# A two-layer graph kernel: edge counts gathered in windows of 12 destinations with four matmuls each, in place of 16 with five

## The chip, the core and the metric

The kernel runs on one NeuronCore of a Trainium2 chip. Its engines are TensorE (PE, with its weight loads PEld), VectorE (DVE), ScalarE (ACT), GpSimd (POOL) and SyncE (SP, which here only issues DMAs). The metric is the time of one execution on the device in microseconds (us).

## What is computed

`x` is 1250 x 1024, and the graph has 41250 edges (20000 random pairs in both directions and one loop per node), sorted by destination.

```python
h = jnp.maximum(_layernorm(x, axis=-1), 0.0)
# twice, with (Ws1, Wn1, b1) and (Ws2, Wn2, b2):
h_neigh = jax.ops.segment_sum(h[src], dst, num_segments=N_NODES)
h = h @ Ws + h_neigh @ Wn + b
# and at the end
x = x + h
```

The segment sum is done as a matrix product. `AT[s, d]` is the number of edges from source s to destination d; with it, h_neigh @ Wn is the transpose of AT times (h @ Wn). So the kernel first has to build AT, 1250 x 1250 small whole numbers, from the edge list.

## The kernel before

**Products.** A 32-bit operand is split in a high and a low part, and each product is three matmuls (high by high, high by low, low by high; `slab_products`, L1067). All are 128 x 128 weights by up to 512 columns.

**Stage 1** makes y1 = h @ Wn1 in 20 results (2 column halves by 10 node tiles), each of 8 slabs of 3 matmuls. The first 8 results are made while x is still being normalized and transposed. Then `stage1_order` goes on with the other 12 results and puts the count matmuls between their slabs: every 3 slabs a group of windows. PE, ACT, DVE and SP each walk an order that is derived from that list.

**From edge list to windows.** SP loads src and dst to `edge_ints`, 125 partitions of 330 edges (L422, L423). DVE splits src into its tile (src >> 7) and its place in the tile (src & 127) and writes f16 rows of 16 values to `edge_f16`: 5 edges a row, as 5 places, 5 tile keys, 5 destinations and one value that isn't used (`cast_edges`, L876 to L886). SP stores these 8250 rows of 32 bytes to `edge_rows` in DRAM (L432). Since the list is sorted, the edges of 16 neighbouring destinations (a window) are one run of rows, and the kernel must find where it begins: DVE compares the first destination of every third row with each window's start (`sample_edges`, L893), PE sums over partitions with 22 matmuls of 80 columns (L1107), and DVE turns the sums into row numbers (`find_rows`, L899 to L901). SP reads these and for each window copies 128 rows from DRAM to `window_edges`, one row per partition (`load_windows`, L442). A fetch is the 8 windows of one load of registers; fetches 0 to 6 are issued in a row, the others between the loads of the second half's weight slabs. POOL makes `pair_m` and `pair_key` from each fetch with four instructions (L602 to L608); a destination outside the window gets a key that matches nothing.

**Counting.** For a pair of windows DVE makes two tables of zeros and ones: `hot_m` (for each of 5 edges per partition, 128 source places; L922) and `hot_n` (10 source tiles by 16 destinations = 160 columns; L924), in a ring of `HOT` = 4 pairs. PE multiplies them: 5 matmuls of 160 columns per window add up to its counts (`count_window`, L1059). Three windows share a PSUM bank, and when such a group is done ACT copies 480 columns to AT (`save_counts`, L735).

In the end DVE and PE sum all counts. If the sum isn't 41250, a slow path that can hold any edge list builds AT anew; `flag` decides, and every engine branches on it before stage 2.

**Later stages.** Stage 2 (L1155, L1163) makes the transposed first layer, PE's L1192 makes the second layer's products by a scheme of sums of blocks, and L1208 multiplies by AT again.

The functions that the diff touches:

## Time and profile before

| | |
|---|---|
| Runs | 663.59, 658.75, 662.05 us, median 662.05 |
| Profiled execution | 660.24 us, span of its trace 658.4 us |
| PE busy in the span | 637.4 us (97%), mean granted clock 0.997 |
| Stretch with the counts, 75.86 to 160.02 us | PE 84.12, weight loads 68.69, DVE 68.34, ACT 27.56, POOL 14.51 us busy |
| Count matmuls | 400 of 128x160, 400 weight loads of 128x128, f16 |

The profiled execution lies inside the spread of the three runs. In the trace a line's "busy" is the time covered by its instructions; the matmuls overlap one another, so the time from one start to the next is shorter than the duration of one. "Idle before" is time in which the engine had nothing to run, with what ended it behind the arrow. PE's idle time adds up to 21 us; nearly all of it lies in the first 23 us, around 171 us and 247 us, and at the end.

### The profile page before, as it was taken

Reading aid. Unit: us, or ns where it says so; the run is one execution under the profiler, and the core shown is the slowest. Engines: PE = TensorE matmul, PEld = TensorE weight load, DVE = VectorE, ACT = ScalarE, POOL = GpSimd, SP = SyncE. Lnnn points to the kernel's source line nnn. Section 1 sums busy time; section 2 is a strip of 40 time slices with the busy share of each in tenths; the row PEclk is TensorE's granted clock in tenths of the full one; section 3 lists DMA queues with packets and bytes.
Section 4 is the critical chain, followed back from the end, with each engine's and each line's share of the span. In section 5 each row is a group of like instructions: output and inputs, shape, how many; then the busy total and the mean of one; then the engine's idle time right before and its main releaser. Section 6 shows DMA issues by size and latency. Waiting matters only on the chain.

```text
span 658.4 us, 8500 instructions
## 1 busy us (share of the span) xinstructions
PE 637.4 (97%) x3280; PEld 555.4 (84%) x3280; DVE 280.3 (43%) x386; ACT 175.7 (27%) x292; POOL 212.4 (32%) x201
## 2 busy tenths in 40 slices
PE   3799999999899999999999999999999999999997
PEld 2688778887799999999999988888888888887885
DVE  2653799783111211120122383325287987611111
ACT  5444343222213313323233121311334433100000
POOL 5432335000247656775680157103214013000000
PEclk9899999999999999999999999999999999999999
DMA  8622330001446766566755766455422243011111
GB/s 276 216 40 56 85 112 33 33 33 62 137 135 196 258 222 232 199 223 202 259 216 176 246 223 231 157 159 160 127 81 69 76 160 96 33 54 59 61 48 62
DMA packets 62724, 90.61 MB, mean 138 GB/s; under 512 B 16545, under 2 KB 34987, under 8 KB 62678
## 3 DMA queue, kind: packets, MB, share of 16 engines
q1 hardware_dynamic: 42342, 76.08, 34.6%
q10 hardware_dynamic: 20336, 13.91, 6.8%
q8 instruction: 30, 0.49, 0.3%
q14 instruction: 16, 0.13, 0.1%
HBM read 58.49 MB, written 31.48 MB: 137 GB/s over the span
## 4 chain that ended last, share of the span: by engine, by line
PE 62%; DMA 1%; DVE 0%; ACT 0%; POOL 0%; issue 0%; SPq 0%; DVEq 0%
PE PS L1192 29%; PE PS L1208 14%; PE PS L1155 10%; PE PS L1163 9%; DMA quarters<-ws_in 1%; DVE W_st L979 0%; POOL prep_sum L617 0%; ACT W_st L728 0%; DVE s L1047 0%; ACT prep L779 0%; SPq L487 0%; DVEq L1046 0%
## 5 line engine op out<-in xcount | busy, mean ns | idle before, releaser
L1192 PE MATMUL PS<-right,left 128*128 128x512 f32 x840 | 190.6, 389 | 0.0
L1192 PEld LDWEIGHTS PS<-right,left 128*128 128x128 f32 x840 | 157.8, 188 | 32.6
L1067 PE MATMUL PS<-W,HT 128*128 128x512 f32 (+1 forms) x480 | 123.0, 406 | 2.5 <-issue 2.4
L1155 PE MATMUL PS<-HT,W_st 128*128 128x416 f32 (+1 forms) x576 | 110.4, 352 | 2.4 <-issue 1.7
L1155 PEld LDWEIGHTS PS<-HT,W_st 128*128 128x128 f32 x576 | 107.9, 188 | 4.0 <-issue 3.1
L1067 PEld LDWEIGHTS PS<-W,HT 128*128 128x128 f32 (+1 forms) x480 | 87.8, 190 | 22.0 <-issue 2.8
L1163 PE MATMUL PS<-AT,y_st 128*128 128x416 f32 (+2 forms) x480 | 92.1, 351 | 0.0
L1163 PEld LDWEIGHTS PS<-AT,y_st 128*128 128x128 f32 (+1 forms) x480 | 90.0, 188 | 0.7
L650 POOL TENSOR_TENSOR left_sum<-h1T 128x640 f32<-128x640 f32 x24 | 41.9, 1746 | 149.9 <-PE PS L1192 120.0
L617 POOL TENSOR_TENSOR prep_sum<-quarters 128x512 f32<-128x512 f32 x40 | 51.6, 1293 | 102.8 <-PE PS L1067 62.8
L1208 PE MATMUL PS<-y_high,AT 128*128 128x512 f32 (+1 forms) x200 | 78.4, 392 | 0.0
L1208 PE MATMUL PS<-y_low,AT 128*128 128x512 f32 (+1 forms) x200 | 78.4, 392 | 0.0
L622 POOL TENSOR_TENSOR prep<-prep_sum,prep 128x512 fp32r<-128x512 f32 x40 | 60.7, 1520 | 25.9 <-ACT prep L779 25.9
L979 DVE TENSOR_TENSOR W_st<-W_st_raw,W_st 128x1024 fp32r<-128x1024 f32 x8 | 14.4, 1798 | 85.2 <-ACT W_st L728 85.2
L1208 PEld LDWEIGHTS PS<-y_low,AT 128*128 128x128 f32 (+1 forms) x200 | 37.2, 186 | 8.8
L1047 DVE TENSOR_TENSOR s<-s,PS 128x512 f32<-128x512 f32 (+1 forms) x20 | 13.7, 687 | 72.0 <-PE PS L1208 72.0
L1208 PEld LDWEIGHTS PS<-y_high,AT 128*128 128x128 f32 (+1 forms) x200 | 37.1, 185 | 8.7
L982 DVE TENSOR_TENSOR y_st<-y_st_raw,y_st 128x1152 fp32r<-128x1152 f32 x8 | 10.9, 1358 | 77.7 <-ACT y_st L765 77.7
L779 ACT ACTIVATE prep<-prep_sum 128x512 fp32r<-128x512 f32 x40 | 23.6, 624 | 64.8 <-POOL prep_sum L617 35.7
L1009 DVE TENSOR_TENSOR s<-s,PS 128x512 f32<-128x512 f32 (+1 forms) x60 | 37.2, 681 | 6.5 <-PE PS L1192 4.5
L924 DVE TENSOR_TENSOR hot_n<-iota_n,pair_key 128x1600 f16<-128x1600 f16 x40 | 39.4, 985 | 0.0
L922 DVE TENSOR_TENSOR hot_m<-iota_m,pair_m 128x1280 f16<-128x1280 f16 x40 | 33.0, 826 | 9.3 <-PE PS L1059 9.2
(79 smaller groups left out, 452.1 us busy)
## 6 DMA issues: line engine op xcount, KB each, us to landing
sums_dram<-prep SPq DMA_DIRECT2D x40, 512.0 KB, 2.9
right<-sums_dram SPq DMA_DIRECT2D x40, 512.0 KB, 3.5
y_dram<-y_out ACTq DMA_DIRECT2D x18, 256.0 KB, 2.1
y_st_raw<-y_dram ACTq DMA_DIRECT2D x8, 576.0 KB
s<-x_in SPq DMA_DIRECT2D x18, 256.0 KB
out<-s SPq DMA_DIRECT2D x18, 256.0 KB
W_raw<-wn_in SPq DMA_DIRECT2D x16, 256.0 KB, 4.0
xin<-x_in SPq DMA_DIRECT2D x8, 512.0 KB, 12.2
```

Of the source, the lines that this page charges most:

```text
L617: nc.gpsimd.tensor_tensor(prep_sum[:, i % PREP, LO, :], quarters[:, QUARTERS.index(a), :], quarters[:, QUARTERS.index(b), :], op).then_inc ...
L622: nc.gpsimd.tensor_tensor(prep[:, i % PREP, LO, :], prep_sum[:, i % PREP, LO, :], prep[:, i % PREP, HI, :].bitcast(F32), ALU.subtract).the ...
L650: nc.gpsimd.tensor_tensor(left_sum[:, k, LO, :], h1_block(*a, k), h1_block(*b, k), op).then_inc(left_summed, 1)
L779: nc.scalar.activation(prep[:, i % PREP, HI, :], prep_sum[:, i % PREP, LO, :], ACT.Copy).then_inc(prep_hi, 1)
L922: nc.vector.tensor_tensor(hot_m[:, u % HOT, :, :, :], iota_m[:, :, :].unsqueeze(1).to_broadcast([P, ROW, P, 2]), pair_m[:, u, :, :].unsque ...
L924: nc.vector.tensor_tensor(hot_n[:, u % HOT, :, :, :], iota_n[:, :, :].unsqueeze(1).to_broadcast([P, ROW, NCOL, 2]), pair_key[:, u, :, :].u ...
L1009: nc.vector.tensor_tensor(c, c, PS[:r, BANKS2[g % 8], :], op).then_inc(dve_evicted, 1)
L1067: ins = nc.tensor.matmul(PS[:r, bank, :], HT[:, a, k, t * P:t * P + r], W[:, k, b, :], start=first and m == 0, stop=last and m == 2)
L1155: ins = nc.tensor.matmul(PS[:, banks[c], 0:w_], W_st[:, a, k, :], HT[:, b, k, o_:o_ + w_], start=k == 0 and m == 0, stop=False)
L1163: ins = nc.tensor.matmul(PS[:, banks[c], 0:w_], y_st[:r, part, s, :].bitcast(dt), AT[:r, s, o_:o_ + w_].bitcast(dt), start=False, stop=s = ...
L1192: ins = nc.tensor.matmul(PS[:, BANKS2[g % 8], :], left[:, k, a, i * P:(i + 1) * P], right[:, KB - 1 - k, b, :], start=k == 0 and j == 0, s ...
L1208: ins = nc.tensor.matmul(PS[:rows_of(t), BANKS2[g % 8], :], AT[:r, s, t * P:t * P + rows_of(t)].bitcast(dt), y.bitcast(dt), start=s == 0 a ...
```

## The change

A window is 12 destinations, and a row holds 4 edges. A window's counts are 4 matmuls of 120 columns (10 source tiles by 12). There are 106 windows and 53 pairs, in groups of 4 windows (480 columns, one bank), 27 groups as before. The last window is empty, since pairs need an even number. Rows of 4 edges don't divide 41250 evenly, so the list is padded to 123 partitions of 84 rows: DVE fills the end with destination 2047 before SP loads, and each of src and dst comes in two DMAs. A fetch is 10 windows (the last one 6), 11 fetches, of which 7 are issued at first and 4 after the last weight slab of the second half. The ring has 5 pairs. `samples` now shares its memory with `src_parts`.

```diff
--- before.py
+++ after.py
@@ -21,25 +21,28 @@
 HI, LO = 0, 1
 PRODUCTS = ((HI, HI), (HI, LO), (LO, HI))
 CH = ((0, 416), (416, 416), (832, 418))
-WIN = 16
-NW = NPAD // WIN
-WPT = P // WIN
-ROW = 5
+WIN = 12
+NW = 2 * -(-N // (2 * WIN))
+FETCH = 10
+NFETCH = -(-NW // FETCH)
+ROW = 4
 ROWX = 16
-EROWS = E // ROW
 SAMPLE = 3
-EP = 125
-EPP = E // EP
-RPP = EPP // ROW
+EP = 123
+RPP = 84
+EPP = RPP * ROW
+TAIL = E - (EP - 1) * EPP
+EROWS = EP * RPP
+NOWHERE = 2047
 NSAMP = RPP // SAMPLE
 KEY = WIN + 2
-ANY = 8
+ANY = 10
 NCOL = NT * WIN
-GROUP = 3
+GROUP = 4
 NG = -(-NW // GROUP)
-HOT = 4
+HOT = 5
 NS = NW // 2
-SPW = WPT // 2
+SPF = FETCH // 2
 SLAB_LAG = 6
 EPS = 1e-5
 EARLY = 8
@@ -151,6 +154,11 @@
     return w // GROUP
 
 
+def fetched(a):
+
+    return range(a * FETCH, min((a + 1) * FETCH, NW))
+
+
 def last_of_group(w):
     return w % GROUP == GROUP - 1 or w == NW - 1
 
@@ -194,16 +202,13 @@
 def sync_order():
 
     ends = y1_ends()
-    yield ("windows", EARLY - 1)
     for p, event in enumerate(stage1_order()):
         if event[:2] == ("y1", NT - 1):
             yield ("slab", event[2])
-            if event[2] == 2:
-                yield ("windows", EARLY)
         if event == ("y1", 2 * NT - 1, 6):
             yield ("w_st", 0)
         if p in ends and ends[p] == NT - 1:
-            yield ("windows", EARLY + 1)
+            yield from (("windows", a) for a in range(EARLY - 1, NFETCH))
 
 
 def scalar_order():
@@ -276,8 +281,8 @@
         ident = at("ident", [P, P], F32, o); o += up(P * 4)
         edge_f16 = at("edge_f16", [EP, RPP, ROWX], F16, o); o += up(RPP * ROWX * 2)
         edge_ints = at("edge_ints", [EP, 2, EPP], I32, o); o += up(2 * EPP * 4)
-        src_parts = at("src_parts", [EP, 2, EPP], I32, o); o += up(2 * EPP * 4)
-        samples = at("samples", [EP, NSAMP, NW], F16, o); o += up(NSAMP * NW * 2)
+        src_parts = at("src_parts", [EP, 2, EPP], I32, o)
+        samples = at("samples", [EP, NSAMP, NW], F16, o); o += up(max(NSAMP * NW * 2, 2 * EPP * 4))
         pad_row = at("pad_row", [P, ROWX], F16, o); o += up(ROWX * 2)
         assert o <= W0, o - W0
 
@@ -337,13 +342,13 @@
 
 
 
-        edges_in = sem("edges_in"); consts_in = sem("consts_in"); b2_in = sem("b2_in")
+        edges_padded = sem("edges_padded"); edges_in = sem("edges_in"); consts_in = sem("consts_in"); b2_in = sem("b2_in")
         x_in_t = [sem(f"x_in_{t}") for t in range(NT)]; x_in_first = sem("x_in_first")
         setup = sem("setup"); pool_self = sem("pool_self"); dve_self = sem("dve_self"); act_self = sem("act_self")
 
         src_split = sem("src_split"); edges_cast = sem("edges_cast"); rows_saved = sem("rows_saved")
         sampled = sem("sampled"); counted = sem("counted"); row_found = sem("row_found")
-        windows_in = [sem(f"windows_in_{a}") for a in range(NT)]
+        windows_in = [sem(f"windows_in_{a}") for a in range(NFETCH)]
         clipped = sem("clipped"); rebased = sem("rebased")
 
         warm = sem("warm"); var_ready = sem("var_ready"); norm_self = sem("norm_self"); norm_ready = sem("norm_ready")
@@ -419,8 +424,12 @@
             load_x_tile(1)
             for k in range(2, KF):
                 load_w(wn1, 0, k)
-            sp.dma_start(edge_ints[:, 0, :], src.rearrange("(p e) -> p e", p=EP)).then_inc(edges_in, 16)
-            sp.dma_start(edge_ints[:, 1, :], dst.rearrange("(p e) -> p e", p=EP)).then_inc(edges_in, 16)
+            sp.wait_ge(edges_padded, 1)
+            for part, ends in enumerate((src, dst)):
+                sp.dma_start(edge_ints[0:EP - 1, part, :],
+                             ends[0:(EP - 1) * EPP].rearrange("(p e) -> p e", p=EP - 1)).then_inc(edges_in, 16)
+                sp.dma_start(edge_ints[EP - 1:EP, part, 0:TAIL],
+                             ends[(EP - 1) * EPP:E].rearrange("(p e) -> p e", p=1)).then_inc(edges_in, 16)
             for t in range(2, NT):
                 load_x_tile(t)
             with nc.allow_non_contiguous_dma("4 KB bias as a column for each feature tile"):
@@ -436,11 +445,10 @@
             def load_windows(a):
 
                 _, rows = nc.values_load_multi_w_load_instructions(
-                    row_i[0:1, a * WPT:(a + 1) * WPT], engines=(mybir.EngineType.SP,), min_val=0, max_val=EROWS,
+                    row_i[0:1, fetched(a)[0]:fetched(a)[-1] + 1], engines=(mybir.EngineType.SP,), min_val=0, max_val=EROWS,
                     skip_runtime_bounds_check_because="a count of sampled edges times 3, less 3 and at least 0: at most EROWS - 3")
-                for j in range(WPT):
-                    sp.dma_start(window_edges[:, a * WPT + j, :],
-                                 edge_rows[bass.ds(rows[j], P), :]).then_inc(windows_in[a], 16)
+                for w, row in zip(fetched(a), rows):
+                    sp.dma_start(window_edges[:, w, :], edge_rows[bass.ds(row, P), :]).then_inc(windows_in[a], 16)
 
             sp.wait_ge(rows_saved, 32)
             sp.wait_ge(row_found, 1)
@@ -588,19 +596,20 @@
                                    allow_small_or_imprecise_dtypes=True).then_inc(iotas, 1)
 
 
-            for a in range(NT):
-                pool.wait_ge(windows_in[a], WPT * 16)
-                rows = window_edges[:, a * WPT:(a + 1) * WPT, :]
+            for a in range(NFETCH):
+                pool.wait_ge(windows_in[a], len(fetched(a)) * 16)
+                these = slice(fetched(a)[0], fetched(a)[-1] + 1)
+                rows = window_edges[:, these, :]
                 place = rows[:, :, 2 * ROW:3 * ROW]
 
                 def in_pairs(field):
                     return rows[:, :, field * ROW:(field + 1) * ROW].rearrange("p (u e) i -> p u e i", e=2)
 
                 def pairs(tile):
-                    return tile[:, a * SPW:(a + 1) * SPW, :, :].rearrange("p u i e -> p u e i")
+                    return tile[:, these.start // 2:these.stop // 2, :, :].rearrange("p u i e -> p u e i")
 
                 nc.gpsimd.tensor_copy(pairs(pair_m), in_pairs(0))
-                nc.gpsimd.tensor_tensor(place, place, win_start[:, a * WPT:(a + 1) * WPT].unsqueeze(2).to_broadcast([P, WPT, ROW]),
+                nc.gpsimd.tensor_tensor(place, place, win_start[:, these].unsqueeze(2).to_broadcast([P, len(fetched(a)), ROW]),
                                         ALU.subtract).then_inc(clipped, 1)
                 pool.wait_ge(clipped, 2 * a + 1)
                 nc.gpsimd.tensor_scalar(place, place, -1.0, float(WIN), ALU.max, ALU.min).then_inc(clipped, 1)
@@ -872,7 +881,7 @@
 
             def cast_edges():
 
-                dve.wait_ge(edges_in, 32)
+                dve.wait_ge(edges_in, 64)
                 nc.vector.tensor_scalar(src_parts[:, 0, :], edge_ints[:, 0, :], P - 1, None, ALU.bitwise_and).then_inc(src_split, 1)
                 nc.vector.tensor_scalar(src_parts[:, 1, :], edge_ints[:, 0, :], P.bit_length() - 1, None,
                                         ALU.logical_shift_right).then_inc(src_split, 1)
@@ -887,7 +896,7 @@
                                         ALU.mult).then_inc(edges_cast, 1)
 
             def sample_edges():
-                dve.wait_ge(edges_cast, 1)
+                dve.wait_ge(edges_cast, 3)
                 dve.wait_ge(setup, 3)
                 first = edge_f16[:, :, 2 * ROW:2 * ROW + 1].rearrange("p (q s) o -> p q (s o)", s=SAMPLE)[:, :, 0:1]
                 nc.vector.tensor_tensor(samples[:, :, :], win_start[:EP, :].unsqueeze(1).to_broadcast([EP, NSAMP, NW]),
@@ -900,6 +909,7 @@
                 chain(nc.vector.tensor_scalar(row_f[:, :], row_f[:, :], 0.0, None, ALU.max))
                 nc.vector.tensor_copy(row_i[:, :], row_f[:, :]).then_inc(row_found, 1)
 
+            nc.vector.memset(edge_ints[96:EP, :, TAIL:EPP], NOWHERE).then_inc(edges_padded, 1)
             statistics(0)
             statistics(1)
             low_of_h(0)
@@ -917,7 +927,7 @@
 
             dve.wait_ge(iotas, 2)
             def one_hots(u):
-                dve.wait_ge(rebased, u // SPW + 1)
+                dve.wait_ge(rebased, u // SPF + 1)
                 dve.wait_ge(hot_free, 2 * u + 2)
                 nc.vector.tensor_tensor(hot_m[:, u % HOT, :, :, :], iota_m[:, :, :].unsqueeze(1).to_broadcast([P, ROW, P, 2]),
                                         pair_m[:, u, :, :].unsqueeze(2).to_broadcast([P, ROW, P, 2]), ALU.is_equal)
```

Where the counts stand on PE, in the middle of results 8 and 9 (results with 98 rows are the last tile's). Before:

```order
L1067 MATMUL PS<-W,HT 128x512 x3
L1067 MATMUL PS<-W,HT 98x512 x3
L1067 MATMUL PS<-W,HT 128x512 x3
L1059 MATMUL PS<-hot_n,hot_m 128x160 x15
L1067 MATMUL PS<-W,HT 98x512 x3
L1067 MATMUL PS<-W,HT 128x512 x3
L1067 MATMUL PS<-W,HT 98x512 x3
```

and now:

```order
L1077 MATMUL PS<-W,HT 128x512 x3
L1077 MATMUL PS<-W,HT 98x512 x3
L1077 MATMUL PS<-W,HT 128x512 x3
L1069 MATMUL PS<-hot_n,hot_m 128x120 x16
L1077 MATMUL PS<-W,HT 98x512 x3
L1077 MATMUL PS<-W,HT 128x512 x3
L1077 MATMUL PS<-W,HT 98x512 x3
```

The groups keep their places between the slabs of L1067 (now L1077); each has one matmul more, of 40 columns less.

The SP queue at the edge list, between the first weight slabs and the other x tiles. Before:

```order
L408 DMA W_raw<-wn_in 128x512 x6
L422 DMA edge_ints<-src_in 125x330
L423 DMA edge_ints<-dst_in 125x330
L413 DMA xin<-x_in 128x1024 x7
L413 DMA xin<-x_in 98x1024
L427 DMA b_sb<-b_in 128x8x1
L430 DMA edge_rows<-pad_row 128x16
L432 DMA edge_rows<-edge_f_66 125x1056
```

and now:

```order
L413 DMA W_raw<-wn_in 128x512 x6
L429 DMA edge_ints<-src_in 122x336
L431 DMA edge_ints<-src_in 1x258
L429 DMA edge_ints<-dst_in 122x336
L431 DMA edge_ints<-dst_in 1x258
L418 DMA xin<-x_in 128x1024 x7
L418 DMA xin<-x_in 98x1024
L436 DMA b_sb<-b_in 128x8x1
L439 DMA edge_rows<-pad_row 128x16
L441 DMA edge_rows<-edge_f_66 123x1344
```

Two DMAs of one partition each stand ahead of x tiles 2 to 9, and the first edge DMA waits for DVE's padding.

The DVE around the first weight slabs of the second half (L931, now L941), where it also makes the tables. Before:

```order
L922 TENSOR_TENSOR hot_m<-iota_m,pair_m 128x1280
L924 TENSOR_TENSOR hot_n<-iota_n,pair_key 128x1600
L922 TENSOR_TENSOR hot_m<-iota_m,pair_m 128x1280
L924 TENSOR_TENSOR hot_n<-iota_n,pair_key 128x1600
L931 TENSOR_TENSOR W<-W_raw,W 128x512
L922 TENSOR_TENSOR hot_m<-iota_m,pair_m 128x1280
L924 TENSOR_TENSOR hot_n<-iota_n,pair_key 128x1600
L931 TENSOR_TENSOR W<-W_raw,W 128x512
L922 TENSOR_TENSOR hot_m<-iota_m,pair_m 128x1280
L924 TENSOR_TENSOR hot_n<-iota_n,pair_key 128x1600
L931 TENSOR_TENSOR W<-W_raw,W 128x512
L922 TENSOR_TENSOR hot_m<-iota_m,pair_m 128x1280
```

and now:

```order
L932 TENSOR_TENSOR hot_m<-iota_m,pair_m 128x1024
L934 TENSOR_TENSOR hot_n<-iota_n,pair_key 128x960
L941 TENSOR_TENSOR W<-W_raw,W 128x512
L932 TENSOR_TENSOR hot_m<-iota_m,pair_m 128x1024
L934 TENSOR_TENSOR hot_n<-iota_n,pair_key 128x960
L941 TENSOR_TENSOR W<-W_raw,W 128x512
L932 TENSOR_TENSOR hot_m<-iota_m,pair_m 128x1024
L934 TENSOR_TENSOR hot_n<-iota_n,pair_key 128x960
L941 TENSOR_TENSOR W<-W_raw,W 128x512
L932 TENSOR_TENSOR hot_m<-iota_m,pair_m 128x1024
L934 TENSOR_TENSOR hot_n<-iota_n,pair_key 128x960
L932 TENSOR_TENSOR hot_m<-iota_m,pair_m 128x1024
```

The first slabs stand at the same places, and from the fourth on a pair more comes before a slab. The tables have 1024 and 960 values a partition where they had 1280 and 1600.

## Rows read from the trace of the kernel before

**Rows 1.** The page, sections 1 and 4: busy shares and the chain of waits by line
```profile
PE 637.4 (97%) x3280; PEld 555.4 (84%) x3280; DVE 280.3 (43%) x386; ACT 175.7 (27%) x292; POOL 212.4 (32%) x201
...
PE PS L1192 29%; PE PS L1208 14%; PE PS L1155 10%; PE PS L1163 9%; DMA quarters<-ws_in 1%; DVE W_st L979 0%; POOL prep_sum L617 0%; ACT W_st L728 0%; DVE s L1047 0%; ACT prep L779 0%; SPq L487 0%; DVEq L1046 0%
```

**Rows 2.** Windows by stage: length, busy us (x instructions), PEclk, DMA share, GB/s
```profile
75.80:160.00 84.20, 84.16 (x635) 68.67 (x635) 68.40 (x84) 27.56 (x70) 14.51 (x8) 1.00 0.17 55
```

**Rows 3.** PE timeline, first and last count groups: start us, us, op xcount
```profile
75.86 1.25 PE L1059 MATMUL PS<-hot_n,hot_m 128*128 128x160 f16 x15
76.90 2.33 PE L1067 MATMUL PS<-W,HT 128*128 128x512 f32 x9
79.07 1.25 PE L1059 MATMUL PS<-hot_n,hot_m 128*128 128x160 f16 x15
...
89.69 2.64 PE L1067 MATMUL PS<-W,HT 128*128 128x512 f32 x9
...
159.34 0.89 PE L1059 MATMUL PS<-hot_n,hot_m 128*128 128x160 f16 x10
```

**Rows 4.** Groups by line and shape, engine PE: xcount, busy us, mean ns, idle before
```profile
L1067 PE MATMUL PS<-W,HT 128*128 128x512 f32 x432 | 111.8, 407 | 2.5 <-issue 2.4
...
L1059 PE MATMUL PS<-hot_n,hot_m 128*128 128x160 f16 x400 | 33.3, 234 | 0.0
...
L1107 PE MATMUL PS<-samples,ones_f 125*1 125x80 f16 x22 | 0.9, 201 | 0.0
```

**Rows 5.** The same view of the weight loads, engine PEld: mean ns behind the busy us
```profile
L1059 PEld LDWEIGHTS PS<-hot_n,hot_m 128*128 128x128 f16 x400 | 27.9, 97 | 7.3 <-issue 6.4 <-DVE hot_n L924 0.8
...
L1107 PEld LDWEIGHTS PS<-samples,ones_f 125*1 125x1 f16 x22 | 0.8, 86 | 0.4 <-issue 0.4
```

**Rows 6.** PE timeline before the counts, from 22 to 39 us
```profile
22.28 1.10 PE L1093 MATMUL PS<-ident,hbuf 128*128 128x128 f32 x8 [3.58 <-ACT hbuf L685]
23.13 5.94 PE L1067 MATMUL PS<-W,HT 128*128 128x512 f32 x18
29.00 0.95 PE L1107 MATMUL PS<-samples,ones_f 125*1 125x80 f16 x22
...
32.16 5.72 PE L1067 MATMUL PS<-W,HT 128*128 128x512 f32 x24
```

**Rows 7.** DVE timeline: early steps, then the start of the one-hots
```profile
18.14 0.69 DVE L859 BATCH_NORM_STATS2 stats<-xin 128x6 f32<-128x512 f32 x1 [4.79 <-DMA xin<-x_in]
...
22.21 1.97 DVE L893 TENSOR_TENSOR samples<-win_start,edge_f 125x1760 f16<-125x1760 f16 x1
...
72.03 0.92 DVE L922 TENSOR_TENSOR hot_m<-iota_m,pair_m 128x1280 f16<-128x1280 f16 x1
...
75.49 0.81 DVE L922 TENSOR_TENSOR hot_m<-iota_m,pair_m 128x1280 f16<-128x1280 f16 x1
76.22 0.98 DVE L924 TENSOR_TENSOR hot_n<-iota_n,pair_key 128x1600 f16<-128x1600 f16 x1
77.12 0.81 DVE L922 TENSOR_TENSOR hot_m<-iota_m,pair_m 128x1280 f16<-128x1280 f16 x1
...
80.40 0.68 DVE L931 TENSOR_TENSOR W<-W_raw,W 128x512 fp32r<-128x512 f32 x1
```

**Rows 8.** POOL timeline: first of the four instructions of the last fetch
```profile
96.67 8.80 POOL L602 COPY pair_m<-window_edges 128x40 f16<-128x40 f16 x1 [7.66 <-DMA window_edges<-edge_rows]
```

**Rows 9.** SP queue timeline: DMA issues, start us, us to issue
```profile
7.45 0.36 SPq L423 DMA_DIRECT2D edge_ints<-dst_in  x1
...
31.69 38.82 SPq L442 DMA_DIRECT2D window_edges<-edge_rows  x64
74.66 4.23 SPq L408 DMA_DIRECT2D W_raw<-wn_in  x3
```

**Rows 10.** DMA issues: KB each, median us from issue to landing
```profile
xin<-x_in SPq DMA_DIRECT2D x8, 512.0 KB, 12.2
```

**Rows 11.** ACT timeline: high part of the first second-half weight slab
```profile
77.70 0.62 ACT L660 ACTIVATE W<-W_raw 128x512 fp32r<-128x512 f32 x1
```

## The prediction

> **What bounds the kernel now.** The windows by stage come first: from 75.8 to 160.0 us PE is busy 84.16 of 84.20 us at full clock, DVE 68.40, ACT 27.56, POOL 14.51 [rows 2]. In the whole span PE is busy 97%, and the chain of waits, from its beginning at 235 us to the end, is nearly all later matmuls [rows 1]. It never reaches the stretch that is changed, so it can't tell what that is worth. What does tell it is that PE idles nowhere in the stretch, and that the work behind it is PE's too, or is released by PE. So a microsecond of PE time taken out moves everything behind it forward, as long as nobody else becomes late.
>
> Then the PE timeline: groups of 15 count matmuls and 9 slab matmuls alternate, a period of 79.07 - 75.86 = 3.21 us [rows 3]. What matters is the pitch, from one start to the next, not the duration. A run of n lasts (n-1) pitches and one duration. At 160 columns, with 0.234 us for one [rows 4]: the runs of 15 and 10 differ by 1.25 - 0.89 = 0.36 us for 5 more, so the pitch is 72 ns [rows 3]. At 80 columns, the sampling: (0.95 - 0.20)/21 = 36 ns [rows 4, 6]. At 512 columns: (5.72 - 0.41)/23 = 231 ns [rows 4, 6]. The three lie on one line of 0.45 ns a column with nothing to speak of as a fixed part. So these pairs of load and matmul are bound by the columns that stream through, not by the weights.
>
> **Count matmuls.** Removed: 400 of 160 columns at 72 ns, 28.8 us. Added: 424 of 120 columns. The trace has no 120-column matmul on 128 columns of f16 weights. The line between 80 and 160 columns gives 36 + 40 x 0.45 = 54 ns, so 22.9 us, a gain of 5.9. By group: 15 x 72 = 1.08 us becomes 16 x 54 = 0.86, 27 groups at the same places among the same slabs, and the period goes from 3.21 to 2.99. Bounds: the 36 ns of the 80-column row would be below even streaming; 72 ns holds if the load of 128 f16 weight columns needs as long as that. The 80-column row can't exclude it, as its weights are one column wide. I take 54, because the f16 load of 128 columns lasts 97 ns against 86 for one column [rows 5], so all but 11 ns of it is latency that the next load overlaps.
>
> Here a rule speaks against the change. The Trainium skill (TensorE: Matmul & The Clock Gate, Back-to-back issue gap) gives about 81 ns for a sustained pair of load and matmul at 128 columns. The trace disagrees: 72 ns at 160 columns. By the rule the sum would be 424 x 81 = 34.3 us, 5.5 more than now; it is a rival below.
>
> **Sampling.** 22 matmuls of 80 columns become 28 of 106. By the same line 106 columns take 36 + 26 x 0.45 = 48 ns: 1.34 us against 0.79, on PE and in no one's shadow, **+0.55 us**. DVE's comparison grows from 1760 to 2968 values: 1.97 us [rows 7] becomes 3.3. Before, it ended at 24.2 and PE reached the sampling at 29.00 [rows 6, 7], so 1.3 us more costs nothing; without that 4.8 us cover it would cost all of it. The next tile's statistics move back with it, but PE needs that tile only after 31 us.
>
> **The front of the SP queue.** Two more DMA issues of 0.36 us each, some 0.45 with their gaps [rows 9], stand ahead of x tiles 2 to 9. Tile 2 matters: DVE waits 4.79 us for it, until 18.14 [rows 7], and PE waits 3.58 us until 22.28 for what is made of it [rows 6]. Later PE is full. So a later landing of tile 2 costs its whole delay: 0.9 us if issue decides, nothing if the DMA engines are the bottleneck. A tile needs 12.2 us from issue to landing [rows 10], so the queue is deep in bytes and these hardly change. I take **+0.2**, ends 0 and 0.9. DVE's padding write runs while it waits for the first x tile, and SP asks for it only near 6.9 us: nothing.
>
> **Windows.** 64 DMAs take 38.82 us to issue, 0.607 each [rows 9]. Seven fetches of 10 are 42.5 us. They begin at 31.69 + 0.55 and end near 74.8; the first second-half weight load went out at 74.66 [rows 9], because it waits for PE anyway. The cover is just used up and each further microsecond moves the weights back. DVE's one-hots stand behind these weights. The other 36 windows come after PE ends results 8 and 9, four periods after the first group, about 88.5 us; at 0.607 they are out by 111, the first ten by 95. DVE can't reach their first pair (35) before 72 + 35 x 1.15 + 8 x 0.7 = 118. POOL's first copy of a fetch can last 8.80 us while DVE works without a pause [rows 8]. Even with that it is done by 105. Nothing.
>
> **One-hots.** Next-start times give 0.73 us for 1280 values and 0.90 for 1600 [rows 7]: 0.53 ns a value and 0.05 fixed. A pair of 1024 and 960 values is 0.59 + 0.56 = 1.15 us, 53 pairs 61 us in place of 40 x 1.63 = 65. PE uses a pair in 1.49 us. DVE starts four microseconds ahead. It will wait for the first weight slab: ACT makes that at 77.7 after the first group's eviction [rows 11], now near 78.1, so DVE stands from about 77.9 to 78.8. Pair 5 is then ready near 80.6, and PE wants it with the third group at 76.4 + 2 x 2.99 = 82.4. Cost nothing; without the cover of 1.8 us, what is over. The 0.3 us that the slab run at 89.69 has over its neighbours [rows 3] stay.
>
> ACT evicts the same 480 columns 27 times. The later stages have the same instructions.
>
> **The sum.** -5.9 + 0.55 + 0.2 = **-5.15 us** on the profiled execution's 660.24 gives 655.1. That execution lies 1.8 under the median of the runs, 662.05, and from the median it would be 656.9. I take **656**, between the two.
>
> **Rivals.**
> *The weight load sets the pitch* (slower than before). Place: the count groups. The sum changes sign where 424 pitches are 28.8 - 0.75 = 28.05 us, at 66 ns. With the pitch left at 72 ns the counts take 30.5 us, +1.7 + 0.75 = +2.4: 662.6 on the profile's base, 664.5 on the median's. For it: no row with this load under 120 columns. Against: 97 against 86 ns. Somewhere between, at 62 ns, it would be -1.8. Chance 0.10.
>
> *The page's pitch of 81 ns*: as a mechanism the same, a longer load, +5.5 + 0.75 = +6.2, 667.4. The row at 72 ns speaks flatly against it. Chance 0.02.
>
> *DVE becomes the bound.* If a table costs the same whatever its length, a pair stays at 1.63 us: 72 + 53 x 1.63 + 8 x 0.7 = 164 us, against 160.0 for the end of the counts before. That is +4, 665. It decides from (154.8 - 72 - 5.6)/53 = 1.46 us a pair. The two rows at 0.73 and 0.90 us say that length counts. A weaker form, weights late behind the windows on SP, costs 1 or 2 us. Chance 0.06.
>
> *Tile 2 late by the issue*: -4.5, 656.7. Chance 0.08.
>
> *The change doesn't do its work*: a window whose edges exceed 512 places would send the kernel to its slow path, 10 rounds of 336 edges with three matmuls of up to 512 columns, over 2000 us more. In the given list the furthest edge of a window is the 470th of 512 places (the 593rd of 640 before), and 2047 matches no window. Chance under 0.01.
>
> The forecast keeps 0.73. Its own uncertainty is 2 ns of pitch (0.8 us) and the base, 4.8 us between the runs. The range of **652.5 to 662.5** holds it, the late tile and half of the floor cases. About 1% is what this measurement can tell from no change, 6.6 us. My gain is 0.8%, so **within 1%** has 0.77, **faster by over 1%** 0.19 (the forecast with a kind base, or DVE's shorter tables freeing something unseen), **slower by over 1%** 0.04 (the page's rule, DVE bound at its worst, the slow path).
>
> **What will show it.** The 120-column runs of 16 in the PE timeline: (duration - one)/15 near 54 ns, period near 2.99 us, counts over some 5.4 us earlier after a start 0.75 later. DVE's tables near 0.65 us each with the wait before the hot tables on PE. The first weight load near 74.8 to 75. The sampling near 1.5 us as a run. I am wrong if the runs of 16 last over 1.2 us (load-bound), if PE shows idle time before L1069 with the hot tables as releaser, or if PE's 3.58 us wait grew.

## The result and the profile after

The changed kernel takes 668.31 us (median of 6 runs, 666.0 to 672.61) against 662.11 for the kernel before. The ratio of the runs is **1.0109**, 95% interval 1.0077 to 1.014 (the two medians alone give 1.0094): slower by about 1%, where 656 us and a gain of 0.8% were forecast, and outside the range of 652.5 to 662.5. The profiled execution has a span of 666.0 us, 7.6 more than before. Three executions in the experiments below, one of e12 (912.48 us at a granted clock of 0.66) and two of the kernel before beside e7 to e12 (671.23 and 2273.64 us), are longer than the others of their kernel, and the ratios leave them out.

First the page of the profile of the changed kernel, section 1 (busy us, share, instructions):

```profile
PE 637.4 (96%) x3310; PEld 553.7 (83%) x3310; DVE 277.3 (42%) x413; ACT 175.4 (26%) x292; POOL 213.8 (32%) x205
```

PE is as busy as before, 637.4 us [rows 1], so the 7.6 us are idle time on PE. What the count matmuls saved in busy time is filled up again, by the longer sampling and by stretches at half clock. Its timeline says where (start us, us, op; in brackets the idle time before, and what ended it):

```profile
26.38 1.97 PE L1103 MATMUL PS<-ident,hbuf 128*128 128x128 f32 x8 [6.04 <-ACT hbuf L694]
...
30.72 0.97 PE L1077 MATMUL PS<-W,HT 128*128 128x512 f32 x3 [0.22 <-POOL W L568]
...
34.21 1.52 PE L1117 MATMUL PS<-samples,ones_f 123*1 123x106 f16 x28
...
81.83 1.04 PE L1069 MATMUL PS<-hot_n,hot_m 128*128 128x120 f16 x16
...
84.83 1.05 PE L1069 MATMUL PS<-hot_n,hot_m 128*128 128x120 f16 x16
...
91.65 0.98 PE L1069 MATMUL PS<-hot_n,hot_m 128*128 128x120 f16 x8 [3.20 <-DVE hot_n L934]
92.39 3.40 PE L1077 MATMUL PS<-W,HT 128*128 128x512 f32 x9
```

Three things are to be seen, besides the counts.

1. The transposes of tile 2 begin at 26.38 us, where they began at 22.28 [rows 6]: PE waited for `hbuf`, 6.04 us in place of 3.58, and the eight then last 1.97 us in place of 1.10, at half clock. After them there are new short waits for POOL, and the sampling starts at 34.21 in place of 29.00. The counts begin at 81.83, not 75.86 [rows 3]: **6.0 us late**.
2. A run of 16 lasts 1.04 us. With 0.22 for one, the pitch is (1.04 - 0.22)/15 = 55 ns, and the period is 84.83 - 81.83 = 3.00 us. Both are what was forecast (54 ns, 2.99 us).
3. In the third group PE stops for **3.20 us** for `hot_n`. Then the clock is at half: 9 slab matmuls last 3.40 us in place of 2.31.

The last count starts at 165.03 us. In the windows, the stretch in which PE waited shows the granted clock:

```profile
88.00:91.60 3.60, 0.45 (x8) 0.28 (x6) 1.87 (x4) 1.81 (x4) 0.61 (x2) 0.96 0.92 304
91.60:94.60 3.00, 2.95 (x13) 2.40 (x14) 3.00 (x6) 2.33 (x5) 0.00 (x0) 0.50 0.13 48
```

(The columns are the stretch and its length, busy us of PE, PEld, DVE, ACT and POOL with their instructions, PEclk, DMA share, GB/s.) PE was busy for 0.45 us of 3.6; for the next three microseconds the granted clock was 0.50, which is 1.2 GHz.

**Why the counts begin late.** The SP queue of the changed kernel:

```profile
6.63 0.61 SPq L429 DMA_DIRECT2D edge_ints<-src_in  x1
7.28 2.13 SPq L431 DMA_DIRECT2D edge_ints<-src_in  x1
9.45 0.25 SPq L429 DMA_DIRECT2D edge_ints<-dst_in  x1
9.74 3.22 SPq L431 DMA_DIRECT2D edge_ints<-dst_in  x1
13.01 3.81 SPq L418 DMA_DIRECT2D xin<-x_in  x8
...
37.95 48.29 SPq L451 DMA_DIRECT2D window_edges<-edge_rows  x70
86.29 12.86 SPq L413 DMA_DIRECT2D W_raw<-wn_in  x8
```

The DMAs behind the two of 122 partitions are held for 2.13 and 3.22 us. The x tiles go out from 13.01, not 7.85. DVE's first use of tile 2, and the two instructions that met next:

```profile
22.24 0.69 DVE L868 BATCH_NORM_STATS2 stats<-xin 128x6 f32<-128x512 f32 x1 [8.68 <-DMA xin<-x_in]
...
26.29 3.23 DVE L902 TENSOR_TENSOR samples<-win_start,edge_f 123x2968 f16<-123x2968 f16 x1
```

```profile
25.00 6.90 POOL L568 TENSOR_TENSOR W<-W_raw,W 128x512 fp32r<-128x512 f32 x3
```

Tile 2 is used at 22.24 us, 4.10 later than at 18.14 [rows 7]. And POOL's last three weight subtractions last 6.90 us, where before they took 5.66:

```profile
20.90 5.66 POOL L560 TENSOR_TENSOR W<-W_raw,W 128x512 fp32r<-128x512 f32 x3
```

PE's last nine products before the sampling stand behind the last of these slabs. They are released by POOL at 31.96 us, 0.06 us after it ends, and the sampling starts 2.31 us after POOL ends; before it was 2.44.

**Why PE stops.** The 70 windows take 48.29 us to issue in place of the 42.5 that I had worked out, from a start 6.3 us later than before. So the first second-half weights go out at 86.29 us, 4.5 after the first count, where before they went out 1.2 ahead of it [rows 3, 9]. What loads the row numbers into SP's registers (duration in ns, min/median/max; first and last start): the second and third load of the changed kernel, and then all ten of the kernel before.

```profile
L447 SPq TENSOR_LOAD <-row_i x1: 2076/2076/2076, 43.0 to 43.0; - x1
```

```profile
L447 SPq TENSOR_LOAD <-row_i x1: 947/947/947, 50.8 to 50.8; - x1
```

```profile
L438 SPq TENSOR_LOAD <-row_i x10: 521/528/740, 30.8 to 89.2; - x10
```

DVE stands in its order behind those weights:

```profile
83.46 0.65 DVE L934 TENSOR_TENSOR hot_n<-iota_n,pair_key 128x960 f16<-128x960 f16 x1
89.73 0.69 DVE L941 TENSOR_TENSOR W<-W_raw,W 128x512 fp32r<-128x512 f32 x1 [5.63 <-ACT W L669]
90.34 0.68 DVE L932 TENSOR_TENSOR hot_m<-iota_m,pair_m 128x1024 f16<-128x1024 f16 x1
90.94 0.65 DVE L934 TENSOR_TENSOR hot_n<-iota_n,pair_key 128x960 f16<-128x960 f16 x1
```

Five pairs were ready at 84.1 us. The sixth comes after 5.63 us of waiting for `W`, and PE runs out of tables. A pair takes 0.60 us from the start of one table to that of the next, and 0.57 more, so 1.17, near the forecast 1.15.

### The profile page after: what moved, and what is told of

Same layout as the page of the kernel before. It is cut to its first block, busy times and chain, and to the rows that moved or that the text cites. A ratio compares the mean times of both kernels' runs of the same rounds, so it can differ in the third digit from the quotient of the medians.

```text
span 666.0 us, 8685 instructions
## 1 busy us (share of the span) xinstructions
PE 637.4 (96%) x3310; PEld 553.7 (83%) x3310; DVE 277.3 (42%) x413; ACT 175.4 (26%) x292; POOL 213.8 (32%) x205
## 4 chain that ended last, share of the span: by engine, by line
PE 54%; POOL 1%; DMA 1%; DVE 0%; ACT 0%; SPq 0%; issue 0%; POOLq 0%; DVEq 0%
PE PS L1202 29%; PE PS L1218 14%; PE PS L1165 6%; PE PS L1173 5%; DMA quarters<-wn_in 1%; POOL prep L631 0%; POOL prep_sum L626 0%; DVE W_st L989 0%; SPq L482 0%; ACT W_st L737 0%; DVE s L1057 0%; ACT prep L788 0%; SPq L495 0%; POOLq L625 0%; DVEq L1056 0%
## 5 line engine op out<-in xcount | busy, mean ns | idle before, releaser
L1077 PE MATMUL PS<-W,HT 128*128 128x512 f32 (+1 forms) x480 | 124.7, 409 | 2.9 <-issue 2.4
L1077 PEld LDWEIGHTS PS<-W,HT 128*128 128x128 f32 (+1 forms) x480 | 88.6, 192 | 23.4 <-issue 2.8
L631 POOL TENSOR_TENSOR prep<-prep_sum,prep 128x512 fp32r<-128x512 f32 x40 | 57.7, 1446 | 28.8 <-ACT prep L788 28.6
L932 DVE TENSOR_TENSOR hot_m<-iota_m,pair_m 128x1024 f16<-128x1024 f16 x53 | 36.5, 690 | 6.7 <-PE PS L1069 6.6
L934 DVE TENSOR_TENSOR hot_n<-iota_n,pair_key 128x960 f16<-128x960 f16 x53 | 34.8, 656 | 0.0
```

The lines of the kernel that those rows point to most:

```text
L631: nc.gpsimd.tensor_tensor(prep[:, i % PREP, LO, :], prep_sum[:, i % PREP, LO, :], prep[:, i % PREP, HI, :].bitcast(F32), ALU.subtract).the ...
L932: nc.vector.tensor_tensor(hot_m[:, u % HOT, :, :, :], iota_m[:, :, :].unsqueeze(1).to_broadcast([P, ROW, P, 2]), pair_m[:, u, :, :].unsque ...
L934: nc.vector.tensor_tensor(hot_n[:, u % HOT, :, :, :], iota_n[:, :, :].unsqueeze(1).to_broadcast([P, ROW, NCOL, 2]), pair_key[:, u, :, :].u ...
L1077: ins = nc.tensor.matmul(PS[:r, bank, :], HT[:, a, k, t * P:t * P + r], W[:, k, b, :], start=first and m == 0, stop=last and m == 2)
```

## The experiments

Ratios are to the kernel before on the same chip, with 95% intervals; like the first one, they can differ from the ratio of the two medians, by up to 0.2%. "Repaired" is short for one DMA each for src and dst and fetches of 8.

### e1 and e2: undo one part each

e1 pads inside each of 125 partitions, so each of src and dst comes in one DMA.

```diff
-EP = 123
+EP = 125
...
-                sp.dma_start(edge_ints[0:EP - 1, part, :], ends[0:(EP - 1) * EPP]...)
-                sp.dma_start(edge_ints[EP - 1:EP, part, 0:TAIL], ends[(EP - 1) * EPP:E]...)
+                sp.dma_start(edge_ints[:, part, 0:REAL], ends...)   # REAL = 330
...
-            nc.vector.memset(edge_ints[96:EP, :, TAIL:EPP], NOWHERE)
+            nc.vector.memset(edge_ints[:, :, REAL:EPP], NOWHERE)
```

> The changed kernel with its edge list padded in another way: 125 partitions of 330 edges as before, each with 6 places of padding behind them (one write of DVE), so that src and dst come in one DMA each and no DMA of one partition is left. Windows, matmuls and fetches are the changed kernel's. Theory 'front': the two one-partition DMAs hold SP's queue for 2.13 and 3.22 us, x tile 2 lands 4.1 us late, and PE begins the counts 6.0 us late. Then the counts begin near 76.6 us (81.83 in the changed kernel), and PE still stalls some 3 us in the third group, as the windows' issue still takes 48 us: about 5.4 us less than the changed kernel, 663. Rival 'more edge work' (larger sampling and casts, more bytes): no change, the counts begin near 82 us, 668.

Measured: 664.05 us, ratio 1.0053 (1.0023 to 1.0082). The x tiles in the SP queue, and PE's timeline:

```profile
7.51 4.45 SPq L418 DMA_DIRECT2D xin<-x_in  x8
```

```profile
30.19 1.52 PE L1115 MATMUL PS<-samples,ones_f 125*1 125x106 f16 x28
...
77.64 1.04 PE L1067 MATMUL PS<-hot_n,hot_m 128*128 128x120 f16 x16
...
87.14 0.98 PE L1067 MATMUL PS<-hot_n,hot_m 128*128 128x120 f16 x8 [2.87 <-DVE hot_n L932]
```

The x tiles go out at 7.51 us and the counts begin at 77.64, 4.2 earlier than in the changed kernel: the front theory holds for 4.2 of its 6.0 us, where 5.2 were expected. The sampling still starts 1.2 us later than at 29.00 [rows 6], though its tile is not late. The stall is there, 2.87 us.

e2 changes one number.

```diff
-FETCH = 10
+FETCH = 8
```

> The changed kernel with fetches of 8 windows (14 fetches, 7 of them first) in place of 10. The one-partition DMAs stay. Theory 'row numbers': SP loads 10 row numbers in 0.94 or 2.1 us where 8 took 0.53, so the windows go out late, the second half's first weights behind them too, and DVE with its tables waits for those weights. Then the loads are back at 0.53, the first 56 windows are out in about 34 us (by 72), the first weight load waits for PE again (near 80.5), PE's 3.2 us stall and the half-clock stretch behind it go: 5.3 us less than the changed kernel, 663, and the counts begin at 81.8 as there. Rival 'DVE is the bound': the stall stays.

Measured: 661.86 us, ratio 1.0014 (0.9986 to 1.0043). The loads of row numbers, the SP queue and PE:

```profile
L447 SPq TENSOR_LOAD <-row_i x11: 522/527/732, 36.5 to 109.4; - x11
```

```profile
37.41 33.81 SPq L451 DMA_DIRECT2D window_edges<-edge_rows  x56
80.38 13.76 SPq L413 DMA_DIRECT2D W_raw<-wn_in  x8
```

```profile
81.58 1.04 PE L1069 MATMUL PS<-hot_n,hot_m 128*128 128x120 f16 x16
...
160.02 0.61 PE L1069 MATMUL PS<-hot_n,hot_m 128*128 128x120 f16 x8
```

The loads are back at 0.53 us, SP waits for PE again, and there is no stall: the last count starts at 160.02, 5.0 us before that of the changed kernel, with the start of the counts all but unmoved (81.58 against 81.83). DVE is no bound. The gain is of the size that the row-number theory gave, but the edit changes two things: with fetches of 8, the seven fetches ahead of the weights hold 56 windows, not 70. At this run's own rate, 33.81/56 = 0.604 us a window, 70 would take 42.3 us (an estimate) and be out near 79.7, just ahead of 80.38. So by that estimate the short loads would have been enough, but no run had 70 windows in front and loads of 8. The next run keeps the 70.

### e6: is it ten numbers, or where they lie?

```diff
-        row_i = at("row_i", [1, NW], I32, o)
+        row_i = at("row_i", [1, NFETCH * 16], I32, o)
...
-                    row_i[0:1, fetched(a)[0]:fetched(a)[-1] + 1], ...
+                    row_i[0:1, a * 16:a * 16 + len(fetched(a))], ...
...
```

> The changed kernel with fetches of 10 windows, but the 10 row numbers of each fetch stored at a multiple of 64 bytes (16 places a fetch, written by two copies on DVE). In the changed kernel the loads of 10 numbers alternate between 2.1 us (starts at an odd multiple of 40 bytes) and 0.94 (at an even one). If the start address makes the 2.1 us, all loads take 0.94 or less, the 70 windows go out in about 43 us instead of 48.3, by 81, the weights come in time and PE's stall of 3.2 us mostly goes: 664. If only the number 10 counts, they stay between 0.94 and 2.1 and so does the time, 668.

Measured: 664.13 us, ratio 1.0056 (1.0027 to 1.0086). The loads and the SP queue:

```profile
L447 SPq TENSOR_LOAD <-row_i x11: 714/945/1623, 36.6 to 117.2; - x11
```

```profile
38.00 44.71 SPq L451 DMA_DIRECT2D window_edges<-edge_rows  x70
82.76 12.33 SPq L413 DMA_DIRECT2D W_raw<-wn_in  x8
```

So both count. Ten numbers at a multiple of 64 bytes take 0.95 us (the median; the shortest is the last fetch of six, the first takes 1.16 and one behind the weights 1.62), eight take 0.53. In the changed kernel all five loads that start at an odd multiple of 40 bytes take over 2 us (three times 2.07 to 2.08, and 3.51 and 2.70 behind the weights), and the six others 0.94 to 1.17. With the same 70 windows in front, the issue is 3.6 us shorter, and PE's waits for hot tables shrink from 3.20 to 0.76 us in all. This is the run that shows the row numbers as the cause of most of the stall, with only the place of the numbers changed.

### e4 and e5: what holds the queue?

e4 puts the two one-partition DMAs at the head of the queue.

```diff
+            for part, ends in enumerate((src, dst)):
+                sp.dma_start(edge_ints[EP - 1:EP, part, 0:TAIL], ends[(EP - 1) * EPP:E]...)
             sp.dma_start(xin[:, 0, 0:HALF], x[0:P, 0:HALF]).then_inc(x_in_first, 16)
...
-                sp.dma_start(edge_ints[EP - 1:EP, part, 0:TAIL], ends[(EP - 1) * EPP:E]...)
```

> The changed kernel with its two one-partition DMAs as the very first in SP's queue, where no transfer is under way. Why do they hold the queue? If by themselves (a cost of the form), the first x tile lands 5 us later than at 3.4, and the time stays near 668 or above. If because they meet a backlog of the W transfers, they take about 0.4 us each, x tile 0 lands at 4.2, x tile 2 near 19, the counts begin near 77.5: 664 (the windows' stall stays).

Measured: 669.17 us, ratio 1.0130 (1.0093 to 1.0167). A miss. The SP queue:

```profile
0.75 0.35 SPq L421 DMA_DIRECT2D edge_ints<-src_in  x1
...
8.26 1.84 SPq L432 DMA_DIRECT2D edge_ints<-dst_in  x1
10.15 7.46 SPq L418 DMA_DIRECT2D xin<-x_in  x8
```

The one-partition DMAs are cheap there, 0.35 us for the first, as the backlog theory has it. But the delay did not go: now the second DMA of 122 partitions is held for 1.84 us, and the eight x tiles take 7.46 to issue. What came behind a DMA of 122 partitions was held in both orders. The one-partition DMAs were only the first to stand there.

e5 splits the last partition off in the kernel before: 124 partitions and 1.

```diff
-            sp.dma_start(edge_ints[:, 0, :], src.rearrange("(p e) -> p e", p=EP))...
-            sp.dma_start(edge_ints[:, 1, :], dst.rearrange("(p e) -> p e", p=EP))...
+            for part, ends in enumerate((src, dst)):
+                sp.dma_start(edge_ints[0:EP - 1, part, :], ends[0:(EP - 1) * EPP]...)
+                sp.dma_start(edge_ints[EP - 1:EP, part, :], ends[(EP - 1) * EPP:E]...)
```

> The kernel before, with src and dst each loaded in two DMAs: 124 partitions of 330 edges, and the last partition by itself. Nothing else is changed. Theory 'front': the two one-partition DMAs alone take 5 us of SP's queue, x tile 2 lands near 22, and the kernel is 4 to 5.5 us slower, 667. Rival: the 5 us come from the padding or the other sizes; then no change, 662.

Measured: 661.37 us, ratio 1.0000 (0.9968 to 1.0031): no change. My first front theory, that the one-partition DMAs cost 5 us by their form, falls. All four issues took 0.25 to 0.48 us.

### e7: 122 partitions by themselves

The kernel before with 122 and 3 partitions.

```diff
...
+                sp.dma_start(edge_ints[0:122, part, :], ends[0:122 * EPP]...)
+                sp.dma_start(edge_ints[122:EP, part, :], ends[122 * EPP:E]...)
```

> The kernel before, with src and dst each loaded in two DMAs: 122 partitions and the other 3. No matmul or window is changed. The run with 124 and 1 partitions held nothing up (four issues of 0.25 to 0.48 us), and with the one-partition DMAs first in the queue it was still the DMA behind a 122-partition one that waited. New theory: the partition count decides over how many DMA engines a transfer is spread; 122 = 2 x 61 leaves two, whose queues fill, and the next issues wait. The Trainium skill (DMA: Bandwidth & Descriptors, How many engines) says so: the largest number up to 16 that divides the count. From the changed kernel's trace, as a mechanism here: the issues behind the 122-partition ones take 2 to 3 us, x tile 2 is used near 22 (18.1 before), the counts begin near 80, and the kernel is 3.5 to 5 us slower, 664 to 665. Rival: it needs the 1344-byte rows or one-partition transfers as well; then no change, 660.5.

Measured: 664.95 us, ratio 1.0055 (1.0028 to 1.0081). The SP queue of e7, then the windows from 12 to 14 us of e7 and of e5:

```profile
7.67 1.73 SPq L425 DMA_DIRECT2D edge_ints<-src_in  x1
...
9.74 3.28 SPq L425 DMA_DIRECT2D edge_ints<-dst_in  x1
13.07 3.89 SPq L413 DMA_DIRECT2D xin<-x_in  x8
```

```profile
12.00:14.00 2.00, 0.83 (x2) 0.76 (x3) 1.07 (x1) 1.98 (x3) 2.00 (x2) 1.00 0.15 53
```

```profile
12.00:14.00 2.00, 0.00 (x0) 0.00 (x0) 1.19 (x1) 2.00 (x3) 2.00 (x2) 1.00 1.02 308
```

The same is seen, 1.73 and 3.28 us, with 1320-byte rows, without padding and without a one-partition transfer. The x tiles go out at 13.07, tile 2 is used 4.16 us late, and the counts begin at 81.31 us, 5.45 late. Most of what is over came with the clock: PE waited 6.77 us for that tile, and the granted clock was 0.50 from 24 to 32 us. In the stretch from 12 to 14 us the DMA engines are nearly idle (the two numbers at the end: share and GB/s), while with 124 + 1 partitions, in the second row, they are full (1.02). The Trainium skill (DMA: Bandwidth & Descriptors, section Why a DMA increments its semaphore by 16 and not by 1) says that a transfer is spread over the largest number of engines up to 16 that divides the partition count; by this rule that is 2 for 122, 4 for 124, 5 for 125. The traces agree as far as they go: the share of 0.15 is 2.4 of 16 engines at work, and the issue waits. They don't name the engines of a packet, so the count of two, and that it is why the issue waits, isn't shown by a trace.

### e9: POOL beside DVE

In the repaired kernel:

```diff
             low_of_h(1)
-            sample_edges()
             for t in range(3, NT):
                 statistics(t)
                 low_of_h(t - 1)
                 if t == 3:
+                    sample_edges()
                     find_rows()
```

> The repaired kernel (one DMA each for src and dst, fetches of 8) with DVE's comparison of samples moved behind the next tile's statistics and low part. In the changed kernels three weight subtractions on POOL take 6.90 us while the comparison of 3.23 us runs, 5.66 beside one of 1.97, and PE waits for them. Theory 'POOL beside DVE': with the comparison at 25.5 to 28.8 the three take 3.8 us, PE isn't held by POOL, waits for the samples instead, and reaches the sampling near 28.9 in place of 30.2 to 31.2: 1 to 2 us less than the repaired kernel, 659. Rival: the subtractions are long by themselves there; then PE comes later, 661 or more.

Measured: 657.62 us, ratio 0.9963 (0.9934 to 0.9991). POOL, and PE:

```profile
21.52 3.85 POOL L566 TENSOR_TENSOR W<-W_raw,W 128x512 fp32r<-128x512 f32 x3
```

```profile
29.52 1.52 PE L1115 MATMUL PS<-samples,ones_f 125*1 125x106 f16 x28 [1.40 <-DVE samples L900]
...
77.05 1.04 PE L1067 MATMUL PS<-hot_n,hot_m 128*128 128x120 f16 x16
```

The three subtractions take 3.85 us with DVE's comparison out of their way; 5.66 us beside one of 1.97, 6.90 beside one of 3.23. All but 0.2 us of the comparison's length is added to them (1.81 and 3.05 us), so POOL made next to no headway while it ran. In the Trainium skill (GPSIMD Engine Reference, section Specifications) the two share their SBUF interfaces, with contention where a DVE instruction has two SBUF inputs, as this one has; the trace agrees. PE now waits 1.40 us for the samples instead. What the edit gains over the repaired kernel is small at best, as e10 and e11 show below.

### e3, e8, e10, e11: both repairs, and what became of the gain

e3 has the edits of e1 and e2 together:

```diff
-EP = 123
+EP = 125
-FETCH = 10
+FETCH = 8
```

> Both edits together: one DMA each for src and dst, and fetches of 8. Front and row numbers together explain the miss: the counts begin near 76.6 us, no stall of PE, the count matmuls 5.9 us shorter: 657 to 658, 0.7% under the kernel before. If something else is lost in the later stages (PE idles 1.45 us at 305 us in the changed kernel and not before), it stays 1.5 us above that, 659.

Measured: 660.64 us, ratio 0.9998 (0.9974 to 1.0023), a miss by about 3 us; no stall in the counts, which begin at 78.65 and end 2.5 us before those of the kernel before. So 2.5 us of gain at that point, and none at the end in these rounds. Two tests of where it went. e8, the kernel before with more rows in DRAM:

```diff
-    edge_rows = nc.dram_tensor("edge_rows", (EROWS + P + 3, ROWX), F16, kind="Internal").ap()
+    edge_rows = nc.dram_tensor("edge_rows", (10332 + P + 3, ROWX), F16, kind="Internal").ap()
```

> The kernel before with 2082 unused rows behind edge_rows in DRAM, so that the tensors behind it (y1_dram, sums_dram) move to the addresses that they have in the changed kernel. Nothing else is changed. Where did the gain of the repaired kernel go? Its counts end 2.5 us before those of the kernel before, and the whole isn't shorter: stage 2 idles more for W_st, and the stores of the prepared sums land in 3.0 to 3.2 us in place of 2.9. Theory 'addresses': this kernel is 1.5 to 3 us slower, 662 to 663. Rival 'chance or phase': no change, 660.5.

Measured: 660.91 us, ratio 0.9996 (0.9972 to 1.002). And e10, e3 with the tensor of the rows declared behind the one of the sums:

```diff
-    edge_rows = nc.dram_tensor("edge_rows", (EROWS + P + 3, ROWX), F16, kind="Internal").ap()
...
+    edge_rows = nc.dram_tensor("edge_rows", (EROWS + P + 3, ROWX), F16, kind="Internal").ap()   # now after sums_dram
```

> The repaired kernel with edge_rows declared behind y1_dram and sums_dram, which keeps those two at fixed addresses whatever edge_rows' size. Theory 'addresses': stage 2's waits for W_st shrink to those of the kernel before (under 1 us in all), 658. Rival 'chance or phase': no change, 660.6.

Measured: 658.51 us, ratio 0.9963 (0.9935 to 0.999). e11 is e3 again, with no edit.

> The repaired kernel (one DMA each for src and dst, fetches of 8) once more, beside the next kernel on one chip. Its first measurement gave 0.9998 of the kernel before, while its counts ended 2.5 us earlier; the kernel with the same stage 1 and edge_rows last gave 0.9963. Theory 'chance': the same matmuls run at one of two pitches (187 or 190 ns in stage 2) and the clock halves after some stalls, differently in each execution, so the ratio lies between 0.996 and 0.999 here. Rival 'addresses or phase': it stays at 1.000.

Measured: 659.23 us, ratio 0.9976 (0.9948 to 1.0005). Since e8 shows nothing, e3, e10 and e11 overlap, and e10's waits for `W_st` add up to 2.0 us where the theory wanted under 1, the address theory has nothing for it. The repaired kernel lies at 0.996 to 1.000.

These three kernels have the same stage 1, and yet their counts begin at 78.65 (e3), 79.08 (e10) and, in e11, at

```profile
77.11 1.04 PE L1067 MATMUL PS<-hot_n,hot_m 128*128 128x120 f16 x16
```

The difference is mostly half clock before the sampling: behind a wait of 1.84 us for POOL, the last nine products took 3.92 us in e3 and 2.37 in e11. So a single trace's start of the counts is good to some 2 us. It also means that e9 shows no gain over the repaired kernel: its counts begin at 77.05, as here, and its ratio is that of e10 on the same chip.

Part of the loss is seen in every trace, PE's waits at the beginning of tiles in stage 2. Two of e11, then one of e3:

```profile
244.81 13.89 PE L1163 MATMUL PS<-HT,W_st 128*128 128x416 f32 x72 [2.00 <-DVE W_st L987]
...
296.68 13.89 PE L1163 MATMUL PS<-HT,W_st 128*128 128x416 f32 x72 [1.56 <-DVE W_st L987]
```

```profile
248.11 15.44 PE L1163 MATMUL PS<-HT,W_st 128*128 128x416 f32 x72 [2.37 <-ACT h1T L777]
```

In e3's execution the clock fell as well: the granted clock was 0.72 in the three microseconds behind this wait and 0.65 behind the one at 169.95 us, and the 72 matmuls took 15.44 and 15.28 us in place of 13.6 to 14.0. Those 3 us are more than its gain of 2.5.

Added over stage 2, the waits behind the first tile are 0.68, 1.30, 0.72 and 0.68 us in the four traces with the old windows (before, e5, e7, e8), and 1.37 to 3.70 in the ten with the new (2.70 in the changed kernel, 3.56 in e11). What makes them longer isn't settled; no run tested it but for the addresses.

### e12: take the wait for the samples away

```diff
                 if t == 3:
                     sample_edges()
+                if t == 4:
                     find_rows()
...
-                    if i == 1 and k == 1:
+                    if i == 1 and k == 3:
                         pe.wait_ge(sampled, 1)
```

> The kernel with the later comparison of samples, and PE's sampling moved two slabs and one tile's transposes further back (find_rows behind the statistics of tile 4). There PE waited 1.40 us for the samples. If that was the last cost of the front, the counts begin near 75.7 us in place of 77.05, as in the kernel before, and end 5.5 us before its: 656, ratio 0.991 to 0.993. Rival: the later row numbers delay the windows or the transposes of tile 4, and PE waits there; then no gain over 657.6.

Measured: 658.6 us, ratio 0.996 (0.9928 to 0.9992). PE doesn't wait for the samples any more:

```profile
23.03 1.97 PE L1102 MATMUL PS<-ident,hbuf 128*128 128x128 f32 x8 [2.71 <-ACT hbuf L692]
24.65 6.49 PE L1076 MATMUL PS<-W,HT 128*128 128x512 f32 x24
...
31.94 1.52 PE L1116 MATMUL PS<-samples,ones_f 125*1 125x106 f16 x28
```

But the counts begin at 77.17, as in e9: in this execution the transposes and part of the 24 products ran at half clock (1.97 us in place of 1.09), which took what the wait had cost. So the forecast of 656 us is missed and a gain over e9 is not shown. e9, e10 and e12 are about 0.4% faster than the kernel before, the best versions found, and no different from one another or from e11 within the intervals.

## Why the prediction was wrong

**The counts: right.** 72 ns became 55 ns a matmul, the period 3.21 became 3.00 us. Of the -5.9 us, 5.3 are seen where nothing stops PE: from the first start to the last end the counts take 84.37 us before and 79.05 in e2. The rivals of a load-bound pitch and of 81 ns (the rule of the Trainium skill named in the prediction) are out.

**The front of the SP queue: the step that failed first.** "I take +0.2, ends 0 and 0.9." I priced the added DMAs at one issue each and took the bytes as unchanged. What I didn't ask is how a transfer is spread: 125 partitions became 122, and that holds the queue for 2.13 + 3.22 = 5.35 us (5.0 in e7, the kernel before with 122 and 3 partitions; with 124 and 1, in e5, nothing). Tile 2 came 4.10 us late. This is the place of the rival "Tile 2 late by the issue" (chance 0.08), at 4.1 us in place of its 0.9. The Trainium skill has the rule, in the section named at e7, and I hadn't weighed it.

**The windows: "0.607 each", failed at nearly the same size.** The 0.607 was a mean of issues and register loads. Eight issues alone take 4.00 us in the trace of before, so 64 are some 32 of the 38.82 us; the rest were eight loads of row numbers at 0.53 us and pauses. Ten numbers cost 0.95 or 2.1, and seven such loads stood ahead of the weights. The text had said that the cover was "just used up and each further microsecond moves the weights back"; with 5.8 us more of issue that came true. The term stood at nothing; the stall of 3.20 us and the half clock behind it cost 4.8 us (the counts take 83.81 us from the first start to the last end, 79.05 in e2). e6, with only the loads shortened, ended the counts 3.6 us earlier; e2, which also moved 14 windows behind the weights, 5.0.

**Sampling: +0.55 on PE was right** (1.52 us against 0.95 as runs), **the "4.8 us cover" wrong.** DVE's result indeed wasn't waited for. But while DVE compares, POOL's weight subtractions make next to no headway, and PE waited for these, as it had before: 1.24 us more on POOL, 1.2 at PE in e1. I had looked for who waits for the instruction and not for who shares something with it.

**One-hots: right**, 1.17 us a pair against 1.15.

**Later stages: "the same instructions".** They are, but their waits grew, which no step held. With the terms as measured, -5.3 + 0.6 + 1.2 + 4.1 + 4.8 = +5.4 us, and the counts end 5.4 us late in the trace. The longer waits for `W_st`, 2.70 - 0.68 = 2.0, bring that to 7.4, where the span shows +7.6; but their cause is open.

The rival that came nearest is the weak form "weights late behind the windows on SP", to which I gave 1 or 2 us inside 0.06. I had no rival in which several covers fail at once, though each of them had been worked out to within a microsecond, and "slower by over 1%" had 0.04. Two of the three signs of being wrong came true: idle time before the counts with the hot tables as releaser, and PE's wait of 3.58 us grown to 6.04.

## What to carry to other kernels

When a change alters the partition count of a DMA, don't price it by bytes or by the number of issues alone: here 124 and 125 partitions held nothing up, and 122 held the queue for 5 us. Split a mean such as "us per transfer" into its instructions before scaling it, above all where the count per load changes. And where a cover is worked out to be used up to the last microsecond, give the case in which it fails its full price and a real chance.

## What the runs showed of the hardware

- A load of 8 neighbouring 4-byte numbers into SP's registers takes 0.53 us, of 10 numbers mostly 0.95 us at a multiple of 64 bytes, and 2.1 us or more where it starts at an odd multiple of 40 bytes.
- Issues behind DMAs of 122 partitions waited 1.7 to 3.3 us on SP and left the DMA engines at a small share for two microseconds; behind DMAs of 124 or 125 partitions nothing waited.
- POOL's subtractions made next to no headway while DVE compared with two SBUF inputs: 3.85, 5.66 and 6.90 us for the same three, beside 0, 1.97 and 3.23 us of it.
- The same 72 matmuls of stage 2 last 13.61 us in some stretches and 13.82 in others of full granted clock, with a change from one to the other at stalls. Over its 8 tiles that can make up to 8 x 0.21 = 1.7 us (an estimate) between two executions of one kernel. These are two rows of e12:

```profile
270.67 13.82 PE L1164 MATMUL PS<-HT,W_st 128*128 128x416 f32 x72
...
321.77 13.61 PE L1164 MATMUL PS<-HT,W_st 128*128 128x416 f32 x72
```
